# Row maxima over all 128 partitions, and the stacked queries and keys reloaded one sequence at a time

## The reference

```python
def attn(x):                       # h = 16 heads of d = 16, g = 4 key groups, s = 256
    q = einsum('bse,hed->bhsd', x, Wq) + bq
    k = repeat(einsum('bse,ged->bgsd', x, Wk) + bk, 4, axis=1)
    v = repeat(einsum('bse,ged->bgsd', x, Wv) + bv, 4, axis=1)
    scores = where(causal, -inf, einsum('bhqd,bhkd->bhqk', q, k) / sqrt(d))
    return einsum('bhqk,bhkd->bhqd', softmax(scores), v)

def ffn(x):                        # weights quantised to -1, 0, 1 times a scale
    return einsum('bse,de->bsd', silu(x @ wu.T) * (x @ wg.T), wd)

x = x + 0.5 * ffn(layernorm(x))
x = x + attn(layernorm(x))
x = x + 0.5 * ffn(layernorm(x))
```

## Time and profile before

| | |
|---|---|
| median of three runs | 662.79 us (662.06 to 664.18) |
| the profiled execution's own time | 661.71 us |
| its span, first to last instruction | 660.0 us |
| mean granted TensorE clock | 0.977 |
| PE busy over the span | 611.0 us (93%) |
| DVE busy | 552.1 us (84%) |
| ACT busy | 361.7 us (55%) |
| POOL busy | 309.4 us (47%) |

### The profile page before, as it was taken

The page is one execution under the profiler, slowest core; times in us unless marked ns, Lnnn a source line. Parts: engine busy times, 40 slices in busy tenths (PEclk is TensorE's granted clock), DMA queues, the critical chain, the costliest instruction groups (busy, mean ns, idle before and its releaser), DMA issues.

```text
span 660.0 us, 13309 instructions
## 1 busy us (share of the span) xinstructions
PE 611.0 (93%) x4276; PEld 339.0 (51%) x4276; DVE 552.1 (84%) x1964; ACT 361.7 (55%) x652; POOL 309.4 (47%) x288
## 2 busy tenths in 40 slices
PE   1688999999898999999999999989898999999998
PEld 1325555555565644545454545434344565556556
DVE  6999888999987768888888787876779999899954
ACT  3434444444345157767777776867775444444442
POOL 6885633541612124646474747464682435334400
PEclk9969999999999879999999999998999999999999
DMA  9410011101205050505050505050020221121201
GB/s 312 157 32 17 17 33 32 32 16 18 33 0 121 1 122 3 122 1 123 2 123 3 122 2 121 3 122 2 2 49 17 62 36 51 49 59 33 65 32 65
DMA packets 48346, 36.52 MB, mean 55 GB/s; under 512 B 33696, under 2 KB 44704, under 8 KB 47776
## 3 DMA queue, kind: packets, MB, share of 16 engines
q1 hardware_dynamic: 48288, 35.80, 22.8%
HBM read 18.22 MB, written 9.44 MB: 42 GB/s over the span
## 4 chain that ended last, share of the span: by engine, by line
PE 51%; DMA 7%; DVE 6%; SPq 3%; issue 3%; ACT 3%; POOL 1%; DVEq 0%; POOLq 0%
PE bank L1023 14%; PE bank L1035 8%; PE bank L1118 7%; PE bank L1145 7%; DMA k_st<-k_scratch 6%; PE bank L1173 6%; PE bank L1182 4%; DVE hl L740 3%; PE bank L1196 2%; PE bank L1187 2%; SPq L228 1%; DVE hid L714 1%; ACT shared L539 1%; SPq L236 1%; PE bank L1156 1%
## 5 line engine op out<-in xcount | busy, mean ns | idle before, releaser
L878 DVE CUSTOM_DVE_ANT_0 sm_out<-bank,mask 128x256 f16<-128x256 f32 (+1 forms) x512 | 157.8, 351 | 45.0 <-PE bank L1145 40.3
L462 ACT ACTIVATE silu<-bank,w_scale 128x512 f32<-128x512 f32 x128 | 87.8, 686 | 169.8 <-PE bank L1023 169.7
L539 ACT ACTIVATE shared<-bank,qk_scale 128x512 f32<-128x512 f32 x192 | 125.7, 682 | 51.2 <-PE bank L1173 49.9
L740 DVE TENSOR_TENSOR hl<-hid,hh 128x512 f16<-128x512 f32 x128 | 142.2, 1111 | 0.0
L1035 PE MATMUL bank<-wT_down,hh 128*128 128x256 f16 x512 | 119.1, 274 | 8.1 <-DVE hl L740 7.5
L1035 PE MATMUL bank<-wT_down,hl 128*128 128x256 f16 x512 | 119.0, 274 | 0.0
L714 DVE SCALAR_TENSOR_TENSOR hid<-silu,h_unit,bank 128x512 f32<-128x512 f32 x128 | 94.7, 740 | 28.2 <-ACT silu L462 24.8
L1023 PE MATMUL bank<-xh,wT_gate 128*128 128x512 f16 x256 | 98.5, 385 | 7.5 <-DVE hid L714 6.8
L1023 PE MATMUL bank<-xh,wT_up 128*128 128x512 f16 x256 | 99.3, 388 | 1.9 <-DVE xl L699 1.9
L1023 PE MATMUL bank<-xl,wT_up 128*128 128x512 f16 x256 | 99.0, 387 | 0.0
L1023 PE MATMUL bank<-xl,wT_gate 128*128 128x512 f16 x256 | 98.8, 386 | 0.0
(11 more groups left out here) (113 smaller groups left out, 827.1 us busy)
## 6 DMA issues: line engine op xcount, KB each, us to landing
q_st<-q_scratch SPq DMA_DIRECT2D x16, 512.0 KB, 5.5
q_scratch<-q_hl SPq DMA_DIRECT2D x8, 512.0 KB, 3.2
out_dram<-x SPq DMA_DIRECT2D x7, 512.0 KB, 2.9
x<-in_x_dram SPq DMA_DIRECT2D x1, 3072.0 KB, 15.1
k_st<-k_scratch SPq DMA_DIRECT2D x32, 64.0 KB, 5.8
x<-in_x_dram SPq DMA_DIRECT2D x2, 512.0 KB, 7.1
shared<-in_w_up_t_dram SPq DMA_DIRECT2D x2, 512.0 KB, 5.1
shared<-in_w_gate_t_dram SPq DMA_DIRECT2D x2, 512.0 KB, 7.2
```

Of the source, the lines that this page charges most:

```text
L462: act.activation(silu[:, e % 2, :], U[e % 2][:, :], ACT.Silu, scale=w_scale[:, 0:1]).then_inc(silu_ready, 1)
L539: act.activation(prob[:, place % 2, i, :], ST[(3 * place + i) % 2][:, :], ACT.Exp, scale=qk_scale[:, 4:5]).then_inc(exp_done, 1)
L740: dve.tensor_tensor(hl[:, par, e, :], hid[:, e % 4, :], hh[:, par, e, :], ALU.subtract).then_inc(hl_ready, 1)
L878: ins = dve.tensor_tensor_reduce(sm_out[:, i, cols], SM[i][:, cols], mask[:, S - size:S], 1.0, MASKED, ALU.add, ALU.max, rowmax[:, seq_par ...
```

## The change

Three things change. `max_scores` reads all 128 rows of `q_st` and `k_st`. For that rows 64 and 65 of `q_st` have to be zero when it runs, so every reload copies the zero rows 66 and 67 over them with one DMA. And a chunk is reloaded in two calls of `read_scratch`, one for each sequence, each with its own semaphore: 2 DMAs of queries, 1 of keys and 1 that clears; for the one DMA of keys, `write_scratch` writes the keys to DRAM twice. The first sequence's reload is issued in the odd sequence's group 1, the second's in group 2.

```diff
-    k_scr = nc.dram_tensor("k_scratch", (2, 2, DH, G, TC), F16)
+    k_scr = nc.dram_tensor("k_scratch", (2, 2, 2, DH, G, TC), F16)
...
-        N_SCR, N_ST = 2, 6
+        N_SCR, N_ST = 3, 4
...
             def write_scratch(c, par):
                 sp.wait_ge(qkv_lo, 3 * c + 3)
-                sp.dma_start(k_scr[par].rearrange("a d g t -> (d g) a t"), k_hl[G * DH:P, :, :]).then_inc(scr_written, 16)
+                for twice in range(2):
+                    sp.dma_start(k_scr[par, :, twice].rearrange("a d g t -> (d g) a t"),
+                                 k_hl[G * DH:P, :, :]).then_inc(scr_written, 16)
                 sp.dma_start(q_scr[par].rearrange("a d h m t -> (d h) a m t"), q_hl[:, :, :, :]).then_inc(scr_written, 16)
-            def read_scratch(c, par):
+            def read_scratch(c, par, seq):
                 sp.wait_ge(scr_written, 16 * N_SCR * (c + 1))
+                cols, loaded = slice(seq * S, (seq + 1) * S), st_loaded[par][seq]
                 for n in range(2):
-                    rows = slice(2 * n * DH, (2 * n + 2) * DH)
-                    sp.dma_start(q_st[rows, par, :, :],
-                                 q_scr[par].rearrange("a d h m t -> (a d) (h m) t")).then_inc(st_loaded[par], 16)
-                    for twice in range(2):
-                        rows = slice((2 * n + twice) * DH, (2 * n + twice + 1) * DH)
-                        sp.dma_start(k_st[rows, par, :, :], k_scr[par, n]).then_inc(st_loaded[par], 16)
+                    sp.dma_start(q_st[2 * n * DH:(2 * n + 2) * DH, par, :, cols],
+                                 q_scr[par].rearrange("a d h m t -> (a d) (h m) t")[:, :, cols]).then_inc(loaded, 16)
+                sp.dma_start(k_st[0:4 * DH, par, :, cols],
+                             k_scr[par].rearrange("a w d g t -> (a w d) g t")[:, :, cols]).then_inc(loaded, 16)
+                sp.dma_start(q_st[64:66, par, :, cols], q_st[66:68, par, :, cols]).then_inc(loaded, 16)
...
                         if odd and g == 1 and not last:
                             write_scratch(c + 2, par)
+                            sp.wait_ge(st_ready, 3 * G * b)
+                            read_scratch(c + 2, par, 0)
                         if odd and g == 2 and not last:
                             sp.wait_ge(st_ready, 3 * G * (b + 1))
-                            read_scratch(c + 2, par)
+                            read_scratch(c + 2, par, 1)
...
                         ins = pe.matmul(SM[i][:, (j - heads[0]) * size:(j - heads[0] + 1) * size],
-                                        q_st[0:4 * DH, par, HPG * g + j, rows:rows + P],
-                                        k_st[0:4 * DH, par, g, at:at + size],
+                                        q_st[:, par, HPG * g + j, rows:rows + P],
+                                        k_st[:, par, g, at:at + size],
                                         start=True, stop=True)
...
-                            if not odd and g == 2:
-                                pe.wait_ge(st_loaded[1 - par], 16 * N_ST * (pair + par + 1))
+                            if g == 2:
+                                pe.wait_ge(st_loaded[1 - par][odd], 16 * N_ST * (pair + par + 1))
```

More of the change, by code:

```diff
@@ L161, in macaron_block @@
         scr_written = sem("scr_written")
-        st_loaded = [sem(f"st_loaded{n}") for n in range(2)]
+        st_loaded = [[sem(f"st_loaded{n}{seq}") for seq in range(2)] for n in range(2)]
         sm_ready, sm_done = sem("sm_ready"), sem("sm_done")
@@ L261, in _ @@
             write_scratch(0, 0)
-            read_scratch(0, 0)
+            read_scratch(0, 0, 0)
+            read_scratch(0, 0, 1)
             load_max(0, 0, 0)
@@ L265, in _ @@
             load_max(0, 0, 1)
-            read_scratch(1, 1)
+            read_scratch(1, 1, 0)
+            read_scratch(1, 1, 1)
             for i in range(NC // 2 - 1):
@@ L1093, in feed_forward @@
                         if t == 0:
-                            pe.wait_ge(st_loaded[0], 16 * N_ST)
+                            pe.wait_ge(st_loaded[0][0], 16 * N_ST)
                         if t < 3:
@@ L1267, in attention @@
             def attention():
+                pe.wait_ge(st_loaded[0][1], 16 * N_ST)
                 max_scores(4, 1, 0)
```

## The result

The changed kernel takes 653.79 us in the median of four runs (652.16 to 657.82), the one before 662.57 in its four: a ratio of 0.987, 95% interval 0.983 to 0.992. It is faster, by 9 us (1.3%) where 28 were forecast, and outside the range. A second set of runs on another occasion gave 651.71 beside 663.61, ratio 0.982 (0.978 to 0.986). Medians are of fast runs alone; of all that follows, only one of the four executions of e2, 679.80 us, was slow and is left out.

What follows compares the result with a forecast made beforehand. The prediction took PE to bound the attention at 32.5 us a chunk. Gains of 15.8 + 3.4 + 2.7 + 1.5 + 4.0 = 27.4 us took 661.7 to 634.3, 635 us as a median; range 625 to 647.

Steps and rivals of the forecast that it cites:

- The mechanism of the gain: On PE, 128*128 `max_scores` lets weight loads go ahead of their matmuls, saving 5.0 us a chunk.
- the rival at 654 us: On PE, weight loads stay late; only reload waits, the clock behind them and the start gain, 9 us; chance 0.08.
- The replacing wait: At the even sequence's step 1, PE waits 1.4 us for the maxima, while the 0.45 us reload wait goes.
- the landing of the maxima "14.2" us after the start of the odd step 1: SP's queue: second-half maxima land behind writes and reads, taken between 13.4 and 14.8 us.
- PE gets there after 14.8 - 2.0 = 12.8 us: First stretch of a chunk: PE, 2.0 us faster, comes for the maxima 12.8 us after the odd step 1 starts.
- the forecast 29.2: Attention's period: a chunk takes 29.2 us, bounds 28.0 and 30.5.
- less far behind: On DVE, `query_low` ends 4.3 us after the odd step 1 starts, instead of 4.57.
- the upper bound: SP's queue: with half the bytes the reads take 5.6 us, so the maxima land by 14.5, or 14.8.
- the third rival: In SP's queue, maxima land at 18.2 us or later, making the kernel slower, about 673 us; chance 0.05.
- The clock: After the five chunks, without the wait ahead, the clock was expected not to fall; 2.7 us off.
- The start: Attention's start: first reload 2.8 us earlier, plus 1.2 for the lower clock, 4.0 us together.
- The friction: In a chunk, 0.6 us added, by choice, because three close limits (27.1, 28.0, 28.6) don't mesh fully.

Runs made afterwards that it cites:

- e2: The changed kernel with `max_scores` back on rows 0 to 63; 673.45 us, ratio 1.013.
- e11: The changed kernel with `max_scores` on rows 0 to 63 and the maxima's two DMAs (half 1) ahead of the first sequence's reads; 652.21 us, ratio 0.983.
- e1: The changed kernel with the maxima's two DMAs (half 1) ahead of the first sequence's reads in SP's queue; 638.93 us, ratio 0.963.
- e4: The changed kernel with `query_low` (second half) on DVE behind the first part of row maxima instead of the third; 639.91 us, ratio 0.964.
- e6: The changed kernel with the maxima's two DMAs issued by POOL, behind the subtraction that makes their data, instead of SP; 644.16 us, ratio 0.972.
- e5: The changed kernel with the maxima ahead of the first reads and `query_low` behind the first part of row maxima; 640.16 us, ratio 0.965.
- e10: The changed kernel with the maxima ahead of the first reads and `query_low` behind the second part of row maxima; 639.64 us, ratio 0.964.
- e8: The kernel before the change with `query_low` (second half) behind the first part of row maxima; 673.17 us, ratio 1.015.

## Why the prediction was wrong

**The mechanism of the gain held.** Loads go ahead across all 128*128 matmuls, the distances are 0.22 and 0.21 us, and the second stretch of a chunk, forecast at 14.2 us, takes 14.5 (270.07 to 284.61). With the queue out of the way the wide matmuls are worth 13.3 us (e11 against e1). The rule on row groups that the prediction takes from the Trainium skill (TensorE: Matmul & The Clock Gate, Part 3) does not hold here: loads of 128*128 go ahead of matmuls of the same row groups in flight. With it falls the rival at 654 us, which the time of the change would fit to the microsecond: the right time for the wrong reason.

**The replacing wait was named, and its size was wrong.** The step that failed is the landing of the maxima "14.2" us after the start of the odd step 1, in the part on the SP queue. They land after 17.8. A second step failed with it, "PE gets there after 14.8 - 2.0 = 12.8 us": PE comes for the maxima after 15.7. So the wait is 2.1 us, not far from the 1.4 forecast, and for the wrong reason; of the 3.2 us by which a chunk is longer than the forecast 29.2, the late maxima make 2.2, which e1 takes away, and PE's late coming 1.0, which stays in e1's 30.2. The pieces of the landing, from the changed kernel's SP queue and DVE, with the odd step 1 at 284.61:

```profile
290.41 1.34 SPq L217 DMA_DIRECT2D k_scratch<-k_hl  x2
291.79 0.77 SPq L219 DMA_DIRECT2D q_scratch<-q_hl  x1
295.04 1.25 SPq L226 DMA_DIRECT2D q_st<-q_scratch  x2
296.34 0.63 SPq L228 DMA_DIRECT2D k_st<-k_scratch  x1
297.01 0.74 SPq L230 DMA_DIRECT2D q_st<-q_st  x1
297.80 1.40 SPq L238 DMA_DIRECT2D q_st<-mx_hl  x2
```

```profile
289.64 0.74 DVE L871 SCALAR_TENSOR_TENSOR q_hl<-bank,b_col,q_hl 128x512 f16<-128x512 f32 x1
```

And DVE in the kernel before, with the odd step 1 at 294.57:

```profile
295.15 0.42 DVE L878 CUSTOM_DVE_ANT_0 sm_out<-bank,mask 128x256 f16<-128x256 f32 x1 [0.40 <-PE bank L1145]
```

| | forecast | measured |
|---|---|---|
| to the end of `query_low` | 4.3 | 5.8 |
| to the first read's issue (third write and landing) | 4.6 | 4.7 |
| to the second maxima DMA's issue | 2.7 | 3.5 |
| to its landing | 2.6 | 3.9 |

- *DVE late by 1.5 us more.* The prediction took DVE to be "less far behind". It is further behind: PE got faster and fills all three banks, so `query_low`, queued behind the row maxima on DVE, comes later after PE's step, not earlier. From the start of the step to the end of `query_low` DVE has no gap now; before, it stood idle for 0.40 us just behind the start, in the last row shown. The same backlog makes PE late: it waits 0.95 us for row maxima and 0.35 for `q_hl` on its way. A backlog on an engine that has become nearly the bound belongs into a loop that passes through its queue. e4 shows that this term is enough: without it the wait is gone.
- *Reads cost SP more.* One of them takes 0.63 us of the queue where 0.45 was taken from the old ones; the prediction carried the old issue time over to a DMA of another form.
- *The landing lies beyond the upper bound* that was built from half the bytes, 14.8. With DVE's delay and the issues taken off, 1.3 us are left over. This chunk has the longest landing of six, 3.9 us; in the others it is 2.9 to 3.3, which would leave 0.3 to 0.7. The bound took half the bytes to need 5.6 us, and they need longer: at the start of the attention the first sequence's reload took 6.8 us from its first issue at 206.74 to the end of PE's wait at 213.58. That is also one of the prediction's own signs of being wrong, reads that land later than 6 us after the writes. Whether full engines, ring order or the runs of 512 bytes make the maxima late behind the reads was not tried; e6, which issues them ahead of the reads, does not tell.

**The period.** 17.84 and 14.54 are 32.4 us, so one loop had taken the place of another of almost the same length (32.5), and five chunks gained nothing. The third rival had the mechanism, with its point at 18.2; the measured 17.8 is 0.4 us short of it. Its chance of 0.05 was far too low, since each of the three terms rested on one row, and DVE's was taken shorter than its row. (The prediction calls it the second rival where it speaks of the runs of 512 bytes; it is the third.) e2 shows its other side: with 64 rows the queue as changed does make the kernel slower, by 10 us.

**The clock** fell where the prediction had it stay, behind waits of 2.5 and 2.9 us: it is part of the chunk of 34.6 us and of the last pair. Such a long wait is not needed for it: in e4 the clock fell twice with no wait of PE over 1.2 us.

**The start** came out at the 4.0 us forecast by luck. PE's wait for the first reload ends 1.5 us earlier (213.58 against 215.08), not 2.8; the clock behind it stayed at 1.00, which is worth some 2.9 us and not 1.2, since PE goes from there to the next eight of `max_scores` in 3.3 us (213.58 to 216.84) where it took 6.1 (215.08 to 221.19). The changed shape has a small part in these 2.9 us, and 0.4 of the sum is lost again before the marker.

**The friction** of 0.6 us, which was a choice, has no test of its own; in e1, with no DMA on the path, a chunk takes 30.2 us where DVE has 28.1 of work, so two such close limits leave 2.1 us, and 29.2 was out of reach even there. By e1's chunk the forecast would have been about 641 us, inside its range.

**What stays open:** which of the remaining waits of e1, DVE's row maxima (0.95 us a chunk), its `q_hl` (0.35) or none by itself, would bring a chunk to DVE's 28 us; e5 and e10 moved only one instruction, and without gain. Open too is what makes the maxima land late behind the reads, and what the clock needs to fall.

## What to carry to other kernels

When a faster engine is forecast, follow each in-order queue once round the whole loop with the engine that will then be behind, and take its backlog as growing. A small transfer that the next step needs must not stand behind large ones that are needed later: two 4 KB DMAs ahead of four reads were worth 15 us, more than the change itself. And moving an instruction earlier on an in-order engine moves its wait in front of all behind it: the same edit gave 14 us in one kernel and cost 10 in the other.

## What the runs showed of the hardware

- A change of matmul shape between 64*128 and 128*128 costs some 0.1 us each way, as the weight load then starts with its matmul (0.31 against 0.22 us behind 512 columns). Over an attention stage of 512 such small matmuls that was 13 us (e11 against e1), with the same columns streamed. By the Trainium skill, TensorEngine Tiling (Array Packing), Key Properties, changing the tiling mode drains the engine; the rows fit that, and give the price.
- A read of 32 partitions in runs of 256 float16 held SP's queue for 0.63 us; one with its 16 KB in a piece held it for 0.37 to 0.42.
- SP's queue orders the issues, not the landings: in the changed kernel the next read was issued at 299.31 us, before the maxima issued ahead of it had landed (302.4). The 4 KB DMAs of the maxima landed 2.9 to 3.9 us after their issue behind four reads (six chunks), and after 1.6 to 3.3, 2.0 in the median, where POOL issued them (e6).
- With PE busy throughout, as in the kernel before, waits put in front of it came out as time (e8: 8.4 us more of waits for row maxima from 200 to 440 us, 10 us more of time).
